# Four layers of cross and self attention on one core: the order of one attend, one subtraction and one eviction in the weighted layer, halves cut into quarters in the first layer, and the mask of the last one written by two matmuls

## The reference

```python
# L0: 16 heads of 8, causal mask over the 77 keys, no output projection
att = softmax(where(causal, Q @ K.T / sqrt(8), -1e9)) @ V
x = layer_norm(att + x);  x = gelu(x @ W1.T + b1) @ W2.T + b2 + x
# L1: scores are multiplied by a given weight and masked by a given mask, per head
att = softmax(where(mask, -inf, (Q @ K.T / sqrt(8)) * weights)) @ V
x = layer_norm(att @ Wo.T + bo + x)
# L2: key mask per batch, then a feed-forward with a second norm
x = layer_norm(attention(x, ctx) + x);  x = layer_norm(relu(x @ w1 + b1) @ w2 + b2 + x)
# L3: self attention in segments of 64 tokens, causal inside a segment, 16 heads of 64,
# with 16 persistent keys and one pooled memory key per head, rotary positions
x = x + self_attention(rms_norm(x)) @ to_out;  x = x + (silu(g) * a) @ ff_w2 + ff_b2
```

## Time and profile before

| | us |
|---|---|
| median of 3 runs | 2436.97 (2435.53 to 2437.94) |
| the profiled execution, its own time | 2442.62 |
| its span, first to last instruction | 2440.8 |

### The profile page before, as it was taken

One profiled execution on the slowest core, in us unless ns is written; L12 is line 12 of the kernel. 1 busy time (PEld: TensorE's weight loads), 2 busy tenths in 40 slices (PEclk: granted clock), 3 DMA queues, 4 the chain that ended last, 5 costly groups with the idle time before them and its releaser, 6 DMA issues.

```text
span 2440.8 us, 83677 instructions
## 1 busy us (share of the span) xinstructions
PE 2287.5 (94%) x27182; PEld 1807.3 (74%) x27182; DVE 1872.0 (77%) x4067; ACT 1474.2 (60%) x3344; POOL 1562.2 (64%) x2374
## 2 busy tenths in 40 slices
PE   7999999988888888999999979999999999999899
PEld 5777778976666666777778967777777777777688
DVE  5888882149999996777775678888888888888566
ACT  5777775548888886888885524444444444444443
POOL 2666663119999995666667766666666666666433
PEclk9999999979999998999999989999999999999999
DMA  4111112235555552222222223333333333333221
GB/s 128 43 43 43 43 45 63 71 90 167 168 167 168 167 157 47 52 50 52 52 50 58 69 72 93 94 96 97 95 94 95 94 94 94 94 94 93 61 62 54
DMA packets 443188, 211.72 MB, mean 87 GB/s; under 512 B 206672, under 2 KB 434000, under 8 KB 442960
## 3 DMA queue, kind: packets, MB, share of 16 engines
q1 hardware_dynamic: 443088, 210.43, 31.9%
HBM read 113.28 MB, written 29.88 MB: 59 GB/s over the span
## 4 chain that ended last, share of the span: by engine, by line
PE 70%; POOL 12%; issue 8%; ACT 4%; DVE 2%; SPq 1%; DMA 1%; POOLq 0%; DVEq 0%; ACTq 0%
PE bank L685 10%; PE bank L1458 9%; PE bank L1418 9%; PE bank L1149 6%; PE bank L702 5%; PE bank L1486 5%; PE bank L659 4%; PE bank L1163 4%; POOL sb_region L1008 4%; ACT sb_pT L771 3%; PE bank L1468 3%; PE bank L1444 3%; POOL sb_rstd L1025 2%; PE bank L1494 2%; POOL sb_z L1029 2%
## 5 line engine op out<-in xcount | busy, mean ns | idle before, releaser
L685 PE MATMUL bank<-sb_ident,sb_region 128*77 128x128 f32 x3072 | 413.0, 278 | 54.0 <-ACT sb_pT L771 50.7
L771 ACT ACTIVATE sb_pT<-bank 77x1024 f32<-77x1024 f32 x384 | 391.8, 1020 | 83.3 <-PE bank L685 82.5
L685 PEld LDWEIGHTS bank<-sb_ident,sb_region 128*77 128x77 f32 x3072 | 349.8, 151 | 107.7 <-issue 104.0
L1548 ACT ACTIVATE sb_l<-sb_l 128x640 f32<-128x640 f32 x128 | 94.5, 738 | 386.6 <-DVE sb_l L1596 386.6
L862 DVE TENSOR_REDUCE sb_max<-bank 128x8 f32<-128x616 f32 x256 | 203.4, 795 | 143.3 <-PE bank L667 74.5
L766 ACT ACTIVATE sb_region<-sb_region 128x616 f32<-128x616 f32 x384 | 276.6, 721 | 22.3 <-POOL sb_region L1008 20.7
L1675 POOL TENSOR_TENSOR sb_pn<-sb_l,sb_r_all 128x512 f32<-128x512 f32 x128 | 134.8, 1053 | 233.0 <-DVE sb_r_all L1606 222.0
L1418 PE MATMUL bank<-sb_region,sb_wqkv 128*128 128x128 f32 x2048 | 253.5, 277 | 6.2 <-DVE sb_region L1584 5.5
L1418 PEld LDWEIGHTS bank<-sb_region,sb_wqkv 128*128 128x128 f32 x2048 | 241.8, 194 | 8.8 <-DVE sb_region L1584 6.1
L1458 PE MATMUL bank<-sb_wvo,sb_region 128*64 128x512 f32 x1024 | 247.9, 605 | 0.0
L867 DVE TENSOR_TENSOR sb_region<-bank,sb_max 128x616 f32<-128x616 f32 x256 | 204.8, 800 | 11.7
(11 more groups left out here) (181 smaller groups left out, 5434.6 us busy)
## 6 DMA issues: line engine op xcount, KB each, us to landing
sb_region<-in_side SPq DMA_DIRECT2D x64, 616.0 KB, 3.8
sb_pT<-sb_region SPq DMA_DIRECT2D x512, 64.0 KB, 2.0
sb_kF<-sb_region SPq DMA_DIRECT2D x512, 64.0 KB, 2.1
scratch_after_A<-sb_y SPq DMA_DIRECT2D x256, 64.0 KB, 1.7
sb_fx<-scratch_after_A SPq DMA_DIRECT2D x96, 128.0 KB, 2.1
sb_mask<-in_mask SPq DMA_DIRECT2D x64, 154.0 KB, 2.3
sb_x<-scratch_after_F SPq DMA_DIRECT2D x128, 64.0 KB, 1.9
sb_ctx<-in_ctxT SPq DMA_DIRECT2D x192, 38.5 KB, 1.8
```

Of the source, the lines that this page charges most:

```text
L685: mm = nc.tensor.transpose(two[0:C, h * T:(h + 1) * T], p_s[b.par][:, head * C:(head + 1) * C], ident[:])
L771: nc.scalar.activation(pT_s[k][:], two[0:C, :], ACT.Copy).then_inc(pT_kept.sem(b), 1)
```

## The change

It has four parts.

1. **A1, order.** PE does the second `attend` of b - 1 behind `transpose_o` and the first-half transposes of P of b. ACT does `keep_att` of b - 1 behind `keep_oT` and behind the second-half exponentials of b. POOL does the first-half shift of b + 1 ahead of `centre` of b - 3 instead of behind it.
2. **A0, quarters.** The transposes of a half are signalled in two quarters of 4 heads, one per bank, and ACT copies each bank with an instruction of 512 columns. The transposes of a quarter wait only for the copy of the bank that they write.
3. **A3, mask.** The mask of a bank is written by one matmul with a stationary operand of 64x128 (the identity twice, `ident2`) instead of two with 64x64, so two matmuls per half instead of four.
4. **Setup.** DVE makes `ident2` with two small copies ahead of F0.

```diff
+        ident2 = sb("ident2", [T, T], BF16)
...
-        pT_made = event("pT_made", CROSS, parts=2)
-        pT_kept = event("pT_kept", CROSS, parts=2)
+        pT_made = event("pT_made", CROSS[1:], parts=2)
+        pT_kept = event("pT_kept", CROSS[1:], parts=2)
+        quarter_made = event("quarter_made", ["A0"], parts=4)
+        quarter_kept = event("quarter_kept", ["A0"], parts=4)
...
+            def transpose_quarters(b, k):
+                pe.wait_ge(exp_made.sem(b), exp_made.count(ph, b, k))
+                for q in range(2):
+
+                    old, old_k = (b, 0) if k == 1 else (b + -1, 1)
+                    if old.exists:
+                        pe.wait_ge(quarter_kept.sem(old), quarter_kept.count(ph, old, 2 * old_k + q))
+                    for h in range(QH):
+                        head = (2 * k + q) * QH + h
+                        mm = nc.tensor.transpose(bank[4 + q][0:C, h * T:(h + 1) * T], p_s[b.par][:, head * C:(head + 1) * C], ident[:])
+                    mm.then_inc(quarter_made.sem(b), 1)
+
             def transpose_p(b, k):
+                if ph == "A0":
+                    return transpose_quarters(b, k)
...
             def attend(b, k, columns=None):
-                pe.wait_ge(pT_kept.sem(b), pT_kept.count(ph, b, k))
+                if ph == "A0":
+                    pe.wait_ge(quarter_kept.sem(b), quarter_kept.count(ph, b, 2 * k + 1))
+                else:
+                    pe.wait_ge(pT_kept.sem(b), pT_kept.count(ph, b, k))
...
                 if has(-1):
                     attend(b + -1, 0, b + 2 if has(2) else None)
+                if has(-1) and ph != "A1":
                     attend(b + -1, 1)
                 if has(-2) and ph != "A0":
                     transpose_o(b + -2)
                 if has(0):
                     transpose_p(b, 0)
+                if has(-1) and ph == "A1":
+                    attend(b + -1, 1)
                 if has(-1):
                     back(b + -1)
...
+            def keep_quarters(b, k):
+                wait_earlier(act, att_made, ph, b, 1, k)
+                for q in range(2):
+                    act.wait_ge(quarter_made.sem(b), quarter_made.count(ph, b, 2 * k + q))
+                    nc.scalar.activation(pT_s[k][:, q * QH * T:(q + 1) * QH * T], bank[4 + q][0:C, :], ACT.Copy).then_inc(quarter_kept.sem(b), 1)
+
             def keep_pT(b, k):
+                if ph == "A0":
+                    return keep_quarters(b, k)
...
                 weighted = ph == "A1"
-                if has(-1):
+                if has(-1) and not weighted:
                     keep_att(b + -1)
                 if has(-2) and ph != "A0":
                     keep_oT(b + -2)
                 if has(0) and weighted:
                     exps(b, 1)
+                if has(-1) and weighted:
+                    keep_att(b + -1)
                 if has(0):
                     keep_pT(b, 0)
...
                     if has(-1):
                         residual(b + -1)
+                    if has(1):
+                        shift(b + 1, 0)
                     if has(-3):
                         centre(b + -3)
-                    if has(1):
-                        shift(b + 1, 0)
                     if has(-3):
                         affine(b + -3)
...
                     rows = slice(r * KH, (r + 1) * KH)
-                    for g in range(T // SEG):
-                        local = bank[4 + r][g * SEG:(g + 1) * SEG, 0:HC * KEYS].rearrange("p (c k) -> p c k", k=KEYS)[:, :, 0:SEG]
-                        nc.tensor.matmul(local, identb[rows, r * KH:(r + 1) * KH], tri[rows, :].rearrange("p (c k) -> p c k", k=SEG),
-                                         start=True, stop=False, skip_group_check=True)
+                    local = bank[4 + r][:, 0:HC * KEYS].rearrange("p (c k) -> p c k", k=KEYS)[:, :, 0:SEG]
+                    nc.tensor.matmul(local, ident2[rows, :], tri[rows, :].rearrange("p (c k) -> p c k", k=SEG),
+                                     start=True, stop=False, skip_group_check=True)
...
+                for r in range(2):
+                    rows = slice(r * KH, (r + 1) * KH)
+                    nc.vector.tensor_copy(ident2[rows, :].rearrange("p (g k) -> p g k", k=KH), identb[rows, rows].unsqueeze(1).to_broadcast([KH, 2, KH]))
                 nc.vector.tensor_copy(tri[:], tri32).then_inc(masks_made, 1)
```

More of the change, by code:

```diff
@@ L855, in half_free @@
             def half_free(b, k):
-                wait_earlier(dve, pT_made, ph, b, 2, k)
+                if ph == "A0":
+                    wait_earlier(dve, quarter_made, ph, b, 2, 2 * k + 1)
+                else:
+                    wait_earlier(dve, pT_made, ph, b, 2, k)
             def peak(b, k):
```

## The result

| | before | after |
|---|---|---|
| median of 3 runs, us | 2436.97 | 2537.62 (2531.91 to 2538.79) |
| profiled execution / its span, us | 2442.62 / 2440.8 | 2538.79 / 2537.0 |
| mean granted clock | 0.985 | 0.973 |

The ratio is 1.0397, with a 95% interval of 1.0378 to 1.0416: slower, by 101 us between the medians and by 96 between the two profiled executions. Forecast were 2506 and a range of 2460 to 2545.

A forecast was written before the change was run, and what follows sets the result against it. POOL, with DVE close behind, was taken to bound A1, PE to bound A3, and PE's copy wait and POOL to limit A0. Terms -8 + 60 + 17 = +69 gave 2506 us; range 2480 to 2525, with rivals 2460 to 2545.

The forecast's parts named there:

- rivals 2 and 3: Both in A1: centring held by the mask, +96 us, chance 0.13; mask not held by the subtraction, +21, chance 0.12.
- Rival 2: A1: DVE's mask holds POOL's centring, batch 7.69 us, +96, in all 2542; chance 0.13.
- A1, the ring: A1: late keep_att closes a one-batch loop of waits, lengthening the batch from 6.15 to 7.11 us, 60 us more.
- the prediction's list: A1: waits from one second-half subtraction's end through exponentials, keep_att, back, project_out and invert to the peak, 2.03 us.
- First-half subtraction at 2.87: A1, POOL: counted from the last second-half subtraction's end, it runs from 2.87 to 4.08 us, taking 1.21.
- Mask at 3.33: A1, DVE: second mask starts at 3.33 us inside POOL's subtraction, is held by +0.62 and ends at 4.73.
- two changes of shape inside PE's idle time: A1, PE: the later second attend costs two stationary-shape changes, 0.1 us each, inside 1 us idle per batch.
- POOL after 4.08 has the centring of 0.80: A1, POOL: after the first-half subtraction the centring takes its usual 0.80 us, so POOL's queue lengthens nothing.
- The term was 60: A1: batch goes from 6.15 to 7.11 us over 62 steps, 60 us more.
- A0, the quarters: A0: copying in quarters removes PE's 0.27 us idle per batch, POOL is late next; 8 us saved.
- the next scores can come forward only by what POOL waited for ACT: A0: the gain is limited to 0.13 us per batch, over some 62 batches 8 us saved.
- A3, the mask: A3, PE: fewer concurrent matmuls save nothing; one more change of stationary shape costs 0.13 us per half, 17 us more.

The follow-up runs named there:

- e2: Kernel before with only A1's order on PE and ACT changed (second attend and keep_att later), POOL's order as before: 2504.7 us, ratio 1.026.
- e5: Kernel before with only ACT's keep_att moved behind the second-half exponentials in A1, PE and POOL as before: 2501.8 us, ratio 1.0245.
- e6: Kernel before with only PE's second attend moved behind the transposes of P in A1, ACT and POOL as before: 2501.5 us, ratio 1.0256.
- e1: Kernel before with only POOL's order in A1 changed, first-half subtraction ahead of the centring: 2464.0 us, ratio 1.0094.
- e3: Kernel before with only A0's quarters: 2426.3 us, ratio 0.9933.
- e8: Kernel before with A0's quarters and, in A0, POOL's key blocks ahead of its centring: 2416.3 us, ratio 0.9906.
- e4: Kernel before with only A3's mask by two wide matmuls per half (and ident2): 2457.6 us, ratio 1.0064.
- e10: Kernel before with A3's masks written twice, wide and narrow matmuls taking turns for each bank: 2521.4 us, ratio 1.0327.
- e12: Changed kernel, in A1 DVE's invert and normalise behind the second peak, PE's back and project_out behind the key and value projections: 2488.8 us, ratio 1.0189.
- e9: Changed kernel with DVE's invert, normalise and keep_v in A1 moved behind the second peak: 2603.9 us, ratio 1.0675.

## Why the prediction was right, and by how much it missed

**Direction and range held, and the size fell to a case that I had put second.** The forecast of 2506 is 32 below the result, and its own range, 2480 to 2525, did not hold; only the one widened by rivals 2 and 3 did. Rival 2, the centring held by the mask, gave 2542 and is 4 off. Its +96 for A1 is the measured 95; that its total comes so near is in part luck, since 9 us too much in its three terms stand against 5 between profile and median, of which the last paragraph of this section speaks.

**A1, the ring: right.** The step of the timeline follows the prediction's list joint by joint. From the end of a subtraction to the next first peak I had 2.03 and the row has 2.01 (701.21 to 703.22). First-half subtraction at 2.87: 2.83. Mask at 3.33, taking 1.40: 3.25, taking 1.45. e2 is this forecast as a kernel: 7.13 for 7.11, +61 for +60. e5 sharpens it: `keep_att` behind the exponentials is enough. e6 adds what the prediction did not see, that the later attend alone closes a second ring of the same length. I had costed it only as two changes of shape inside PE's idle time.

**A1, the centring: wrong, and more than the whole miss.** The step that failed is "POOL after 4.08 has the centring of 0.80". It takes 1.34, in the changed kernel and in e1. With it the affine passes end at about 6.4 in place of 5.9, behind the second peak (5.82 measured), so POOL's queue and not the peak releases the second-half subtraction, and the batch is 7.68 (rival 2: 7.69). The term was 60 and measured 95, where the sum missed by 27. I gave this case 0.13 because a mask that began inside the centring was not longer. That row answers another question: who pays depends on which of the two began first. Rows 9 and the subtraction of 1.44 in the earlier trace rows had already shown that either engine can be the one that pays, and a bound from those should have weighed more. The Trainium skill, SBUF — State Buffer, section "SBUF: two separate sides", says that of a DVE operation with two SBUF inputs and a GpSimd one that reads SBUF, whichever starts first gets the shared port pair for its whole instruction and the other is blocked. The trace agrees for a centring begun inside a mask (+0.54) and disagrees for a mask begun inside a centring (0.78, +0).

**A0, the quarters: right, sized too small.** I had 8 saved and the phase has 14, e3 alone 17. The cause was as told: PE's wait for the copy is gone and POOL's key blocks are late next. The step that was too tight is "the next scores can come forward only by what POOL waited for ACT", 0.13; the batch is 0.21 shorter. Scores that come earlier also bring forward the statistics with which POOL's queue begins; that reading is argued, while e8, where the key blocks stand earlier in the queue and 8 us more are gained, shows that the queue was the limit.

**A3, the mask: right.** 17 were expected and 15 measured (e4: 14). Fewer matmuls saved nothing, since they ran side by side; the stretch from mask to scores grew by 0.08, and the phase by 0.12 per half (15.3 / 128) where the prediction has 0.13; where the other 0.04 lies was not followed. The Trainium skill, TensorEngine Tiling (Array Packing), section Key Properties, says that a change of the tiling mode drains TensorE; e10 agrees in that every change costs time, about 0.10 us, while a drain as such is not to be seen in the rows.

**The sum.** -8 + 60 + 17 = +69 was forecast, -14 + 95 + 15 = +96 is what the traces hold. The other 5 of the 32 lie between profile and median: the profiled execution was 5.6 above the median before and is 1.2 above it now.

## What to carry to other kernels

When a step is moved behind a wait, follow it round until it meets itself: of the four parts the dearest was a copy of 0.4 us that stood behind an exponential, and it cost 60 us although no engine was given any more work. Where two engines hold each other at SBUF, price every new pair in both orders, because a row that shows one order free says nothing of the other, and such a hold costs its full length as soon as it lies on a ring. Test the parts one by one before they go in together: here one part of four was worth having, and with one more line moved it gave 25 us.

## What the hardware showed that was not expected

- **A small one-input operation on POOL is held by DVE's mask.** The centring (128x128, 0.80 us) takes 1.34 in every batch in which it begins while the mask runs, 0.67 past the mask's end (705.24 to 706.58, mask to 705.91). So it is in the traces of all fourteen kernels: 256 centrings began inside a mask, and every one took 1.34 or 1.35. In the other order neither pays: 380 masks began inside a centring, and every one took 0.79. A reading that would fit is that the centring touches SBUF's shared side only early in its 0.80 us; none of these masks began in its first 0.33, so no run here tests it.
- **Of mask and subtraction the later one waits, but the subtraction counts from 0.17 us behind its recorded start.** In e12 a mask that began 0.16 into a subtraction took its usual 0.79 and the subtraction 2.03; in the step of the changed kernel, begun 0.42 into it, the mask took 1.45 and the subtraction its usual 1.22. In the fourteen traces, masks begun 0.03 to 0.04 into a subtraction never paid (12), those begun 0.17 or more into it always did (869), and of the 20 between 0.162 and 0.169, all in e12, 12 did not and 8 did. The one that pays waits for the whole of the other: a held mask ends 0.65 behind the subtraction, a held subtraction 1.08 behind the mask. The rows of e12, from its timeline, one of either kind:

```profile
664.56 1.22 POOL L1046 TENSOR_TENSOR sb_region<-sb_region,sb_max 128x616 f32<-128x616 f32 x1
...
664.73 1.70 DVE L921 SCALAR_TENSOR_TENSOR sb_region<-sb_mask,sb_region 128x616 f32<-128x616 uint8 x1
...
699.60 2.03 POOL L1046 TENSOR_TENSOR sb_region<-sb_region,sb_max 128x616 f32<-128x616 f32 x1
...
699.77 0.79 DVE L921 SCALAR_TENSOR_TENSOR sb_region<-sb_mask,sb_region 128x616 f32<-128x616 uint8 x1
```

- **The longer ring came with a lower clock, the shorter one did not.** Granted is 0.93 over A1 where it was 0.99. From 600 to 900 us it is 0.94 in the changed kernel, and 1.00 in e2, e5 and e6 with their batch of 7.1. In the step below, behind 1.77 us of idle PE, it was 0.50 from 711 to 714 us, the lower level, 1.2 GHz: eight transposes took 1.92 where they take 1.04. From the timeline of the changed kernel:

```profile
703.58 1.04 PE L702 MATMUL bank<-sb_ident,sb_region 128*77 128x128 f32 x8
...
709.98 0.43 PE L736 MATMUL bank<-sb_ident,sb_region 128*128 128x128 f32 x2 [1.77 <-ACT sb_region L849]
...
711.47 1.92 PE L702 MATMUL bank<-sb_ident,sb_region 128*77 128x128 f32 x8
```

  It cost the changed kernel little, since PE was not what the ring waited for most: of 55 distances between batches 52 are 7.62 to 7.72 and three are 7.98 to 8.16. In e9, with a clock of 0.82 over part of A1, its share isn't known.
